# Expert layer: gate and up projections with the weights as the stationary operand

## The reference

```
probs = softmax(x @ Wr + br);  top_w, top_idx = top_k(probs, 1)
g = x @ Wg[e];  u = x @ Wu[e]          # 256 -> 1024, for each expert e
h = silu(g) * u
y = h @ Wd[e]                          # 1024 -> 256
out = y[top_idx] * top_w
```

## Time and profile before

| | |
|---|---|
| median of 3 runs | 701.62 us (699.9 to 705.38) |
| profiled execution | 697.13 us |
| its span, first to last instruction | 695.5 us |
| mean granted TensorE clock | 0.94 of full |
| busy: PE, weight load, DVE, ACT, POOL | 83%, 50%, 60%, 47%, 17% |

### The profile page before, as it was taken

The page is one execution under the profiler, slowest core; times in us unless marked ns, Lnnn a source line. Parts: engine busy times, 40 slices in busy tenths (PEclk is TensorE's granted clock), DMA queues, the critical chain, the costliest instruction groups (busy, mean ns, idle before and its releaser), DMA issues. The chain is left out here.

```text
span 695.5 us, 15435 instructions
## 1 busy us (share of the span) xinstructions
PE 576.1 (83%) x5113; PEld 346.3 (50%) x5147; DVE 414.1 (60%) x947; ACT 325.3 (47%) x592; POOL 119.0 (17%) x161
## 2 busy tenths in 40 slices
PE   3799999999879999796487877875299999999992
PEld 1344555555546655353354444543156666666661
DVE  1676898899853434342789999996423333333331
ACT  2455777777743234244467777763022222222220
POOL 4211212214311000000000000000203333322221
PEclk9987999999999999998589999997599999999997
DMA  8854555545820000007545565660101111111110
GB/s 293 208 120 121 133 118 123 131 118 127 162 62 2 1 1 0 1 1 179 162 105 143 139 148 139 151 145 23 39 9 46 45 45 41 31 38 38 46 31 3
DMA packets 29415, 60.30 MB, mean 87 GB/s; under 512 B 5989, under 2 KB 16647, under 8 KB 26952
## 3 DMA queue, kind: packets, MB, share of 16 engines
q1 hardware_dynamic: 20624, 25.68, 12.5%
q0 software_dynamic: 6432, 18.46, 12.5%
q10 hardware_dynamic: 2328, 15.75, 9.4%
HBM read 58.75 MB, written 7.81 MB: 96 GB/s over the span
## 5 line engine op out<-in xcount | busy, mean ns | idle before, releaser
L1266 DVE TENSOR_REDUCE nmax<-PB 128x2 f32<-128x512 f32 x128 | 85.7, 682 | 22.9 <-PE PB L822 21.1
L532 ACT ACTIVATE probs<-PC 128x512 f32<-128x512 f32 x128 | 74.1, 609 | 22.3 <-PE PC L834 21.3
L751 ACT CAST probs<-PC 128x1024 bf16<-128x1024 f32 x19 | 19.2, 1012 | 113.7 <-PE PC L1177 95.3
L1678 DVE TENSOR_TENSOR probs<-PC,probs 128x1024 bf16<-128x1024 f32 x19 | 23.3, 1225 | 80.8 <-ACT probs L751 71.4
L1169 PE MATMUL PA<-arena,probs 128*128 x227 | 54.2, 390 | 7.5 <-issue 3.7
L822 PE MATMUL PB<-small 64*128 64x256 bf16 x256 | 52.1, 294 | 6.3 <-DVE nmax L1266 6.0
L1188 PE MATMUL PD<-arena,probs 128*128 x456 | 53.1, 273 | 2.5 <-issue 2.5
L1169 PE MATMUL PB<-arena,probs 128*128 x210 | 48.6, 379 | 0.9
L447 POOL DMA_DIRECT2D arena<-in_w_all x16 | 8.5, 532 | 234.6 <-DVE arena L1515 138.3
L1188 PEld LDWEIGHTS PD<-arena,probs 128*128 128x128 bf16 x456 | 44.4, 98 | 8.3 <-issue 3.4
L834 PE MATMUL PC<-small 64*128 64x256 bf16 x256 | 46.7, 284 | 0.7 <-DVE small L1282 0.5
(11 more groups left out here) (208 smaller groups left out, 1130.4 us busy)
## 6 DMA issues: line engine op xcount, KB each, us to landing
arena<-idx_low ACTq DMA_DIRECT2D x15, 1024.0 KB
wst<-in_w_all SPq DMA_DIRECT2D x48, 256.0 KB, 2.7
arena<-in_w_all POOLq DMA_DIRECT2D x16, 384.0 KB, 5.5
arena<-in_idx_all SPq DMA_DIRECT2D x1, 2176.0 KB, 9.8
arena<-in_cond SPq DMA_DIRECT2D x16, 128.0 KB, 7.4
small<-in_x SPq DMA_DIRECT2D x16, 128.0 KB, 10.2
arena<-idx_low POOLq DMA_DIRECT2D x2, 1024.0 KB, 14.5
tok_r<-rows SPq DMA_DIRECT2D x1, 2048.0 KB, 14.3
```

Source lines behind the costliest of these rows:

```text
L532: nc.scalar.activation(probs[:, c, o], PC[:, o], ACT.Exp, scale=SCALE0).then_inc(S["ex"], 1)
L1266: v.tensor_reduce(nmax[:, c, s, :], PB[:, s * 512:(s + 1) * 512].rearrange("p (a k) -> p a k", k=T), AX.X, ALU.max, negate=True).then_inc( ...
```

## The change

The operands of gate and up change places. Stationary is a block of 128 columns of the weights, moving the turned token tile (128 columns). Each of the 8 blocks f of a projection takes 2 x 3 matmuls, so 48 matmuls of 128 columns and 48 weight loads instead of 12 and 12; the result stands with hidden columns on the partitions, as down() wants it. The transposes (turn_h), the semaphore hT and the use of PC go. The BF16 parts h_high and h_low are taken from hh in SBUF. On ScalarE the rounding of slot j comes after the SiLU of slot j and the high part of the next input; on VectorE the remainder of slot j comes after result(j - 1).

```
-                for n in range(2):
+                for f in range(FT):
                     k = 0
                     for kt in range(KT):
-                        o = bass.ds(e * (KT * FF) + (kt * FF + n * 512), 512)
+                        o = bass.ds(e * (KT * FF) + (kt * FF + f * P), P)
                         xo = slice(kt * P, (kt + 1) * P)
-                        for v, w in ((xT_hi, w_hi), (xT_hi, w_lo), (xT_lo, w_hi)):
-                            ins = mm(bank[:, n * 512:(n + 1) * 512], v[:, par, xo], w[:, o], start=(k == 0), stop=(k == 3 * KT - 1))
+                        for w, v in ((w_hi, xT_hi), (w_hi, xT_lo), (w_lo, xT_hi)):
+                            ins = mm(bank[:, f * P:(f + 1) * P], w[:, o], v[:, par, xo], start=(k == 0), stop=(k == 3 * KT - 1))
                             k += 1
-            def turn_h(j):
-                pe.wait_ge(S["hm"], j + 1)
-                unless_first(pe, S["hTl"], j)
-                for f in range(FT):
-                    ins = pe.transpose(PC[:, f * P:(f + 1) * P], hh[:, f * P:(f + 1) * P], ident)
-                ins.then_inc(S["hT"], 1)
...
-            def h_high(j):
-                act.wait_ge(S["hT"], j + 1)
+            def rounded(j):
+                act.wait_ge(S["hm"], j + 1)
                 unless_first(act, S["y"], j)
-                nc.scalar.copy(hT_hi, PC[:]).then_inc(S["hTh"], 1)
+                nc.scalar.copy(h_high, hh).then_inc(S["hTh"], 1)
             def tile(j, par, more=True):
-                h_high(j - 1)
                 gate(j)
                 if more:
                     x_high(j + 1, 1 - par)
+                rounded(j)
...
             def hidden(j):
                 dve.wait_ge(S["gs"], j + 1)
                 dve.wait_ge(S["uu"], j + 1)
-                unless_first(dve, S["hT"], j)
+                unless_first(dve, S["hTh"], j)
+                unless_first(dve, S["hTl"], j)
                 v.tensor_tensor(hh, PB[:], gs, ALU.mult).then_inc(S["hm"], 1)
-            def h_low(j):
+            def remainder(j):
                 dve.wait_ge(S["hTh"], j + 1)
                 unless_first(dve, S["y"], j)
-                v.tensor_tensor(hT_lo, PC[:], hT_hi, ALU.subtract).then_inc(S["hTl"], 1)
+                v.tensor_tensor(h_low, hh, h_high, ALU.subtract).then_inc(S["hTl"], 1)
...
+            def tile(j, par, half, back, more=True, before=True):
                 hidden(j)
                 if more:
                     x_low(j + 1, 1 - par)
-                result(j - 1, 1 - par, half, back)
+                if before:
+                    result(j - 1, 1 - par, half, back)
+                remainder(j)
```

More of the change, by code:

```diff
@@ L267, in program @@
         gs, hh = probs[:, 0, :], probs[:, 1, :]
-        hT_hi, hT_lo = (probs[:, 2, n * 512:(n + 1) * 512].bitcast(BF16) for n in range(2))
+        h_high, h_low = (probs[:, 2, n * 512:(n + 1) * 512].bitcast(BF16) for n in range(2))
         xT_hi, xT_lo = (probs[:, 3, n * T:(n + 1) * T].bitcast(BF16).rearrange("p (n t) -> p n t", n=2) for n in range(2))
@@ L288, in program @@
             "rv", "r", "rx", "rp", "te", "slot", "rows", "asel", "bsel", "inv", "tokn",
-            "xld0", "xld1", "res0", "res1", "tT", "th", "tl", "gu", "gs", "uu", "hm", "hT", "hTh", "hTl", "y", "yo", "so0", "so1")
+            "xld0", "xld1", "res0", "res1", "tT", "th", "tl", "gu", "gs", "uu", "hm", "hTh", "hTl", "y", "yo", "so0", "so1")
         def unless_first(engine, semaphore, count):
@@ L757, in tile @@
                     x_high(j + 1, 1 - par)
+                rounded(j)
             x_high(0, 0)
-            gate(0)
-            x_high(1, 1)
+            tile(0, 0)
             tile(1, 1)
@@ L768, in _ @@
                 tile(j, j % 2, j + 1 < SLOTS)
-            h_high(SLOTS - 1)
         @block.tensor
@@ L1186, in down @@
                     o = bass.ds(e * (FT * T) + f * T, T)
-                    for v, w in ((hT_hi, wd_hi), (hT_hi, wd_lo), (hT_lo, wd_hi)):
+                    for v, w in ((h_high, wd_hi), (h_high, wd_lo), (h_low, wd_hi)):
                         ins = mm(PD[:, 512:512 + T], v[:, f * P:(f + 1) * P], w[:, o], start=(k == 0), stop=(k == 3 * FT - 1))
@@ L1196, in tile @@
                 gate_up(j, par, expert_of(j), PA, wg_hi, wg_lo, "gs", "gu")
-                turn_h(j - 1)
                 gate_up(j, par, expert_of(j), PB, wu_hi, wu_lo, "hm", "uu")
@@ L1213, in _ @@
                 tile(j, j // 2, j % 2, j + 1 < SLOTS)
-            turn_h(SLOTS - 1)
             down(SLOTS - 1, expert_of(SLOTS - 1))
@@ L1696, in tile @@
                     x_low(j + 1, 1 - par)
-                result(j - 1, 1 - par, half, back)
+                if before:
+                    result(j - 1, 1 - par, half, back)
+                remainder(j)
+            x_low(0, 0)
+            tile(0, 0, 0, False, before=False)
             tile(1, 1, 0, False)
@@ L1705, in _ @@
                 tile(j, j % 2, (j - 1) // 2, True, j + 1 < SLOTS)
-            h_low(SLOTS - 1)
             result(SLOTS - 1, (SLOTS - 1) % 2, (SLOTS - 1) // 2, True)
```

## The result

The changed kernel takes 772.49 us (median of 4 runs, 770.24 to 774.84) against 702.15 (4 runs, 699.9 to 705.38): a ratio of 1.0998, 95% interval 1.094 to 1.1057. It is 10% slower. The profiled execution took 770.24 us, its span 768.5.

The account below looks back on a forecast made before the run. TensorE's array bounds the kernel before, its sequencer the changed one. Loop +71, first tile +2, tail -1 make +72 us: 769 on the profiled run, 774 on the median, put at 772; own range 764 to 792, 8-in-10 range 752 to 795.

Parts of the forecast that it names:

- steps 2 and 4: Gate and up: 32 sequencer addresses per projection, 4.1 us, become the bound; tile 13.3 us against 9.39, +71 us.
- step 1: Gate and up on the array: 48 pairs 0.057 us apart, 2.7 us against 2.6, +0.15 per projection if array-bound.
- step 3: Transposes removed: 0.87 us of array time per tile, giving back nothing within the loop under a sequencer bound.
- step 6: First tile: gate loses nothing at the lower clock; up goes from 2.75 to 4.1 us and its expert load shows: +2.
- step 7: Tail: the last rounding can begin when down(17) ends, without 1.04 us of transposes before it: -0.9.
- step 5: Rounding and remainder moved to SBUF: h(j) ready about 6 us after up(j), needed some 13 us after; cost nothing.
- (a): Rival: gate and up addresses don't multiply or cost nothing, array-bound and faster, -15, 686 us; chance 0.11.
- (b): Rival: weight loads set gate and up's pace, upper bound +56, 757 us; about 728 by the skill's 81 ns; chance 0.05.
- (c): Rival: TensorE's clock falls as well in the expert stage, 15.8 us per tile, +115, 815 us; chance 0.05.
- (d): Rival: slower instruction supply in the larger loop, one or two 1.1 us stalls per round, +8 to 15; no separate chance.

Follow-up runs that it names:

- experiment 1: Changed kernel with gate and up always on expert 0's weights, at constant addresses: 684.75 us, 0.9771 of the kernel before.
- experiment 4: Kernel before, operands not exchanged and transposes kept, its 512-column matmuls cut into four of 128 columns: 773.13 us, 1.1043 of the kernel before.
- 6: Changed kernel with only the up projection on expert 0's constant addresses: 726.61 us, 1.0413 of the kernel before.
- experiment 7: Changed kernel with one address per gate and up matmul, 48 per projection instead of 32, and one more expert-number load per projection: 872.1 us, 1.2493 of the kernel before.
- 8: Changed kernel with one load of the expert's number for gate and up together instead of two: 758.71 us, 1.0835 of the kernel before.
- experiment 3: Kernel before with gate and up unchanged but transposes removed, h entering down unturned (result not the reference's): 677.92 us, 0.9649 of the kernel before.
- experiment 9: Changed kernel, complete, branching per tile into one of four constant-address copies of gate and up: 824.32 us, 1.1823 of the kernel before.

## Why the prediction was right

The forecast was 772 us, measured 772.49, and the profiled execution 770.24 against 769 by the sum. That the two agree to half a microsecond is luck: 772 was put between 769 and 774, the runs themselves lie between 770.24 and 774.84, and the difference is 70.3 us by the medians and 73.0 by the spans, against +72. What is not luck is the path to it. Three rows of the chain of the kernel before, which the steps use:

```profile
510.52 2.76 PE PA L1169 x12
...
678.10 0.89 PE PC L1177 x8
...
681.49 2.82 PE PD L1188 x24
```

These are gate(1), the last transposes (they begin as down(17) ends) and down(18). Step by step:

- **The bound (steps 2 and 4).** Predicted 0.128 us per address, 4.1 us per projection, 13.3 us per tile; measured 0.129, 4.2 and 13.22. Experiments 1 and 4 show the cause from both sides, 6, 7 and 8 its size at other counts. From the first matmul of gate(1) to the end of down(17) it was 514.55 to 751.95, 237.4 us, against 510.52 to 678.10, 167.6: +69.8, where the sum had +71. The sum kept the sequencer's other work at 14.39 us for two tiles. Measured, it is 26.45 less 96 x 0.130, 14.0 us: the work of the transposes, which also goes, was not taken off, and an address is a little dearer than 0.128. The two nearly cancel.
- **The array's side (step 1).** 0.057 us per pair forecast, 0.056 measured once the addresses are away (experiment 1), and +0.09 per projection (2.68 against 2.59 us) for +0.15. The Trainium skill's 81 ns ("TensorE: Matmul & The Clock Gate", "Back-to-back issue gap") is not borne out by this stream, which is the case it describes.
- **Transposes (step 3).** No gain behind a sequencer bound: shown by experiment 4 against the changed kernel, 773.13 and 772.49 us. Worth 22 us under an array bound (experiment 3).
- **First tile (step 6).** Start of gate(0) to start of gate(1): 503.38 to 514.55 is 11.2 us, before 501.66 to 510.52, 8.9: +2.3 for +2. **Tail (step 7).** End of down(17) to the start of the last down is 751.95 to 754.56, 2.6 us, against 678.10 to 681.49, 3.4: -0.8 for -0.9. Within the first tile gate(0) did lose a little, 4.75 us for 4.46, and up(0) took 4.30, not 4.1.
- 69.8 + 2.3 - 0.8 = 71.3 of the spans' difference of 73.0; the rest is that the stage began 1.7 us later, in work that the change doesn't touch.
- **Hidden work (step 5).** Right: rounding 1.05 us (from 620.35) and remainder 1.23 (to 622.65), 6 us after up(j) ends at 616.66, as forecast; down(j) begins only at 630.96.
- **Rivals.** (a) is out by the count of 1216 addresses, (b) by experiment 1. (c) did not happen in the changed kernel, whose stage shows 1.00. In experiment 7, with matmuls 0.130 us apart, the granted clock was 0.83, and in the round shown there it cost nothing: the 115 us that (c) charged took no account of a sequencer that is the bound. (d) did not show at this loop size: 25 instruction packets for 20, and a loop branch of 0.21 us as before. Experiment 9 puts its price per miss, taken as 1.1 us, three to four times too low. With one branch of 3.6 us in each of 7 rounds the forecast would have been 797 us (an estimate from that row), just outside the range.
- **The range.** Its lower bound is given as 764, but its own terms (697.13 + 68 + 2 - 1) make 766. It changes nothing here.

## What to carry to other kernels

Before cutting matmuls into more and smaller ones, count what each needs from the sequencer: every distinct slice whose address hangs on a run-time register cost 0.13 us here, and that is hidden only while the array's work for the same stretch takes longer (three matmuls of 256 columns for two addresses were nearly enough, three of 128 were not). Look in the trace for the sequencer's own instructions and its waits: a sequencer that waits 2 us per tile has about that much lead to spend (16 more addresses, 2.1 us, already cost 0.4 us per tile). Removing array work, here the transposes, pays only while the array is the bound. Copies with constant addresses did not pay here, with branches of 3 to 4.6 us; whether they do where the code is already fetched was not tried.

## What the runs showed of the hardware that was not expected

- A long branch of TensorE, one that in all likelihood waits for its code: mostly 3.1 to 4.6 us, against 0.2 us in a small loop (experiment 9).
- The sequencer keeps its pace while the array is at the lower clock: in experiment 7 its addresses from 613.9 to 614.8 are 0.124 to 0.130 us apart, where down() runs at a granted clock of 0.62 (610.4 to 614.7).
- Neither the number of matmuls that share an address nor its operand matters to its spacing: about 0.13 us on average (0.129 to 0.132) in every kernel here, on the matmul as on the weight load. The one exception is down() in experiment 3, 0.157 us, where the array is the bound.
- GpSimd's scatter takes 1.8 us instead of 1.0 in every kernel in which VectorE's remainder is computed right after result() from SBUF, and 1.0 in those with the order of before. The last tiles of the changed kernel, remainder and scatter, then a scatter of the kernel before:

```profile
753.12 1.23 DVE L1668 TENSOR_TENSOR probs<-probs 128x1024 bf16<-128x1024 f32 x1 [0.65 <-ACT probs L751]
753.30 1.93 POOL L469 DMA_INDIRECT out<-probs,tokn  x1 [9.62 <-DVE probs L1675]
...
758.71 1.02 POOL L469 DMA_INDIRECT out<-probs,tokn  x1 [3.48 <-DVE probs L1675]
```

```profile
679.45 1.01 POOL L469 DMA_INDIRECT out<-probs,tokn  x1 [6.76 <-DVE probs L1685]
```

The first 18 scatters start while a remainder runs and end 0.89 to 0.91 us after it ends, though they take from 1.76 to 1.94 us. The last one has no remainder beside it and takes 1.02. It looks as if the scatter did nothing until the remainder was over. In the kernel before the scatter at 679.45 was not slowed by the remainder that began at 680.05, but that one read PSUM and began after it; which of the two matters was not isolated. The scatter is off the critical path.
